# Linear attention and a mixture of experts on one core: the start of the pipeline and the last group rearranged

## The reference

```
q, k = exp(split_heads(x Wq' + bq)), exp(split_heads(x Wk' + bk));  v = split_heads(x Wv' + bv)   # 16 heads of 8
kv = cumsum(k outer v);  k1 = cumsum(k)
out = (q . kv) / sum(q * k1);   x = layernorm(x + merge_heads(out) Wo' + bo)
s = sigmoid(x gate_w');  choice = s + gate_bias;   4 groups of 8 experts: keep the 2 groups
    with the largest sum of their top 2, then the top 8 experts; weights s / sum(s) * 2.5
routed = sum over the 8 chosen of weight * down_e( silu(gate_e x) * up_e x )      # 32 experts, width 64
shared = down_s( silu(gate_s x) * up_s x )                                         # width 128
x = layernorm(x + routed + shared)
```

## Time and profile before

| | us |
|---|---|
| median of 3 runs | 462.77 (462.74 to 463.14) |
| the profiled execution | 463.29 |
| its span in the profile | 461.5 |
| PE busy in the span | 424.0 (92%) |
| DVE, POOL, ACT busy | 347.4, 282.4, 273.3 |

### The profile page before, as it was taken

How to read it: one execution, slowest core, us unless ns; L and a number is a source line. 1 busy time by engine, 2 the same in 40 slices (tenths; PEclk the granted TensorE clock), 3 DMA queues, 4 the chain that set the end, 5 groups by cost and what they waited for, 6 DMA issues and landing times.

```text
span 461.5 us, 10791 instructions
## 1 busy us (share of the span) xinstructions
PE 424.0 (92%) x3954; PEld 324.8 (70%) x3954; DVE 347.4 (75%) x909; ACT 273.3 (59%) x530; POOL 282.4 (61%) x208
## 2 busy tenths in 40 slices
PE   5855799999999999999999999999999999899982
PEld 3733587778867787778877787778877787578761
DVE  2678548797878968797878968796878968777652
ACT  3835334963587546963587546963587546555642
POOL 2565236864676557864677557764677557757781
PEclk9989589999999999999999999999999999999996
DMA  7400544346440823446340923446440913466500
GB/s 233 187 1 1 147 92 90 92 97 141 93 113 7 197 69 82 91 103 135 91 116 12 202 68 74 90 104 134 91 116 9 200 41 81 91 134 129 121 11 23
DMA packets 28660, 45.08 MB, mean 98 GB/s; under 512 B 1984, under 2 KB 10304, under 8 KB 28224
## 3 DMA queue, kind: packets, MB, share of 16 engines
q1 hardware_dynamic: 28608, 44.40, 41.2%
HBM read 41.77 MB, written 2.62 MB: 96 GB/s over the span
## 4 chain that ended last, share of the span: by engine, by line
PE 40%; DVE 32%; issue 12%; POOL 8%; ACT 2%; DVEq 1%; ACTq 0%; POOLq 0%
PE bank L326 39%; DVE units L866 7%; POOL units L958 5%; DVE stats L741 2%; DVE hidden_lo L721 2%; POOL rstd L977 2%; DVE top_of_group L782 2%; DVE x L753 2%; DVE bank L775 1%; ACT hidden_hi L584 1%; DVE replaced L814 1%; DVE out_sb L878 1%; DVE k_sum L847 1%; DVE probs L731 1%; DVE kv_blocks L836 1%
## 5 line engine op out<-in xcount | busy, mean ns | idle before, releaser
L958 POOL TENSOR_TENSOR units<-units,weight_wide 128x512 f32<-128x512 f32 x128 | 174.3, 1367 | 130.5 <-DVE units L866 115.9
L602 ACT ACTIVATE units<-bank 128x512 f32<-128x512 f32 x136 | 80.7, 594 | 79.2 <-PE bank L326 78.9
L866 DVE TENSOR_TENSOR units<-bank,units 128x512 f32<-128x512 f32 x136 | 92.9, 683 | 35.1 <-PE bank L326 28.0
L584 ACT ACTIVATE hidden_hi<-units 128x512 fp32r<-128x512 f32 x136 | 86.1, 634 | 53.7 <-POOL units L958 47.7
L721 DVE TENSOR_TENSOR hidden_lo<-units,hidden_hi 128x512 fp32r<-128x512 f32 x112 | 97.7, 873 | 19.6 <-ACT hidden_hi L584 18.8
L326 PE MATMUL bank<-x_hi,gate_hi 128*128 128x512 f32 x136 | 62.1, 457 | 2.0 <-DVE units L866 1.6
L326 PE MATMUL bank<-hidden_hi,down_hi 128*128 128x512 f32 x136 | 55.0, 404 | 1.7 <-DVE hidden_lo L721 1.7
L326 PE MATMUL bank<-x_hi,up_hi 128*128 128x512 f32 x136 | 54.7, 403 | 1.8 <-ACT units L602 1.8
L326 PE MATMUL bank<-x_lo,gate_hi 128*128 128x512 f32 x136 | 54.6, 401 | 0.0
L326 PE MATMUL bank<-x_hi,gate_lo 128*128 128x512 f32 x136 | 54.4, 400 | 0.0
L326 PE MATMUL bank<-x_hi,up_lo 128*128 128x512 f32 x136 | 54.1, 398 | 0.0
(11 more groups left out here) (107 smaller groups left out, 670.8 us busy)
## 6 DMA issues: line engine op xcount, KB each, us to landing
weight_wide<-weight_d SPq DMA_DIRECT2D x62, 512.0 KB, 6.7
xT<-xT_in SPq DMA_DIRECT2D x8, 256.0 KB, 6.8
x_tok<-x_in SPq DMA_DIRECT2D x8, 256.0 KB, 6.9
out_dram<-out_sb SPq DMA_DIRECT2D x8, 256.0 KB, 2.3
weight_wide<-up_in SPq DMA_DIRECT2D x1, 1088.0 KB, 9.0
up_raw<-up_in SPq DMA_DIRECT2D x1, 1088.0 KB, 11.0
down_raw<-down_in SPq DMA_DIRECT2D x1, 1088.0 KB, 13.2
weight_d<-weightT SPq DMA_DIRECT2D x8, 64.0 KB, 1.6
```

The lines of the kernel that those rows point to most:

```text
L584: nc.scalar.activation(hidden_hi[place(n, g)][:, :], units[place(n, g)][:, :], ACT.Copy).then_inc(hidden_hi_done, 1)
L602: nc.scalar.activation(units[place(n, g)][:, :], up_banks[2 * n % 3][:, :], ACT.Silu).then_inc(silu_done, 1)
L866: V.tensor_tensor(units[place(n, g)][:, :], up_banks[(2 * n + 1) % 3][:, :], units[place(n, g)][:, :], ALU.mult).then_inc(gated_done, 1)
L958: G.tensor_tensor(units[place(n, g)][:, :], units[place(n, g)][:, :], weight_wide[:, (n - 1) % (2 * PIECE), :], ALU.mult).then_inc(hidden_ ...
```

## The change

Four things change in the prologue. The scans of f = 1 (`k_totals(1)`) move on DVE from slot 8 of mid to slot 14, behind the routing and the first two gated products, and `q_times_totals(1)` moves on POOL from slot 10 to slot 13. POOL makes the low parts of the gate and up weights in two pieces each (nine blocks, then eight), and PE's first `up` waits for the first pieces only. Block 0's high and low parts move from slot 1 to slot 2. PE gets products into the output bank that nobody reads (`keep_warm`), 6 + 2 + 1 + 4 + 1 + 3 + 2 of 256 columns at seven places ahead of its waits.

In the steady state `masked_states(f)` moves ahead of `k_totals(f)`, both now in slot 14 (for f > 1). In the group without front (m = 7) the transpose of the routing exponentials moves on PE from slot 10 to slot 11.

In the last group the shared block comes last, the routed ones one slot earlier, and weight pieces 2 and 3 are loaded in slots 4 and 7. Its tail goes in two halves: two `yT` copies, two pairs of transposes into two banks, two residual additions, and in the end ACT normalises two tiles and DVE the two others, each half with a store of its own.

```
+EARLY_BLOCKS = 9
+WARM = {"x1": 6, "x1T": 2, "up": 1, "weight": 4, "den": 3, "between": 2}
         def ready_blocks(n, g):
-            if g == 0 and n in (2, 3):
-                return (1, 2) if n == 3 else ()
+            if g == 0 and n in (1, 2, 3):
+                return ((), (0,), (1, 2))[n - 1]
+        def block_at(n, g):
+            return n if g < GROUPS - 1 else (n + 1) % BLOCKS
...
@@ SP
-                if ffn and n in (5, 9):
-                    load_wide(2 + (n - 5) // 4, g, u)
+                late = (5, 9) if g < GROUPS - 1 else (4, 7)
+                if ffn and n in late:
+                    load_wide(2 + late.index(n), g, u)
+                if g == GROUPS and n == 8:
+                    for h, (done, count) in enumerate(((last_done, 1), (out_done, 2 * GROUPS - 1))):
...                                                  # one store for tiles 2, 3, then one for tiles 0, 1
@@ PE
-                if g == 0 and n == 0:
-                    pe.wait_ge(gate_split, 2)
-                    pe.wait_ge(up_split, 2)
+                if g == 0 and n in (0, EARLY_BLOCKS):
+                    pe.wait_ge(gate_split, 2 if n == 0 else 3)
+                    pe.wait_ge(up_split, 2 if n == 0 else 3)
+            def keep_warm(count):
+                for _ in range(count):
+                    mm(y_bank[:, 0:256], wqT, attn_w[:, 0:256])
...     # called: up(1), up(2) of group 0 ("up"); m = 0: ahead of the waits for x1 (slot 9), x1T (10), the expert
...     # weights (14); m = 1: after the wait for q times totals (slot 0, "den"), ahead of slot 2 ("between")
-                if mid and not front and n == 10:
+                if mid and not front and n == (10 if m == 0 else 11):
                     turn_exponentials(m)
@@ DVE
-                if m == 0 and mid and n == 8:
+                if m == 0 and mid and n == 14:
                     k_totals(1)
+                if front and f > 1 and n == 14:
+                    masked_states(f)
                 if front and f != 1 and n == 14:
                     k_totals(f)
-                if front and f != 1 and n == 15:
+                if front and f == 0 and n == 15:
                     masked_states(f)
+            def last_rows(t, u):                     # for the last group, in slot 4
+                for h, c in enumerate(HALVES):
+                    dve.wait_ge(y_turned, t + 1 + h)
+                    V.tensor_tensor(out_sb[half h], (work_bank, o_bank)[h][:, c], x1[u][half h], ALU.add)
...                                                  # bn_stats of the half; then aggregate, variance, negated mean
+                dve.wait_ge(rstd2_done, t + 1)
+                for i in (2, 3):
+                    last = V.tensor_scalar(out_sb[:, i, :], out_sb[:, i, :], mean_var2[:, i, 0:1], rstd2[:, i:i + 1],
+                                           ALU.subtract, ALU.mult)
+                last.then_inc(last_done, 1)
@@ POOL
-                if mid and m == 0 and n == 10:
+                if mid and m == 0 and n == 13:
                     q_times_totals(1)
                 if g == -2 and n == 16:
                     rows_and_bias(0)
-                    G.tensor_tensor(gate_lo[:, :], gate_raw, gate_hi[:, :].bitcast(F32), ALU.subtract
+                    weight_lows(gate_lo, gate_raw, gate_hi, gate_split, EARLY_COLS)
+                    weight_lows(up_lo, up_raw, up_hi, up_split, EARLY_COLS)
+                    weight_lows(gate_lo, gate_raw, gate_hi, gate_split, LATE_COLS)
-                if g == -1 and mid and n == 7:
-                    G.tensor_tensor(up_lo[:, :], up_raw, up_hi[:, :].bitcast(F32), ALU.subtract
+                if g == -1 and mid and n == 9:
+                    weight_lows(up_lo, up_raw, up_hi, up_split, LATE_COLS)
```

More of the change, by code:

```diff
@@ L27 @@
 RING = 4
+EARLY_BLOCKS = 9
+EARLY_COLS, LATE_COLS = slice(0, 128 * EARLY_BLOCKS), slice(128 * EARLY_BLOCKS, 128 * BLOCKS)
+WARM = {"x1": 6, "x1T": 2, "up": 1, "weight": 4, "den": 3, "between": 2}
+HALVES = (slice(0, GROUP // 2), slice(GROUP // 2, GROUP))
 OUT_SLOTS = (7, 8)
@@ L257, in slot @@
                     sp.dma_start(down_raw, down_d).then_inc(down_loaded, 16)
-                if tail and n == 8:
+                if g == GROUPS and n == 8:
+                    for h, (done, count) in enumerate(((last_done, 1), (out_done, 2 * GROUPS - 1))):
+                        tiles, at = slice(2 - 2 * h, 4 - 2 * h), (GROUPS - 1) * GROUP + 256 * (1 - h)
+                        sp.wait_ge(done, count)
+                        sp.sem_inc(apart, 1)
+                        sp.dma_start(out_d[at:at + 256, :].rearrange("(a p) c -> p a c", p=128),
+                                     out_sb[:, tiles, :]).then_inc(out_stored, 16)
+                if tail and n == 8 and g < GROUPS:
                     t = g - 1
@@ L367, in down @@
                     pe.wait_ge(y_copied, reached(g))
-                cols, h = slice(128 * n, 128 * n + 128), place(n, g)
+                cols, h = slice(128 * block_at(n, g), 128 * block_at(n, g) + 128), place(n, g)
                 mm(y_bank[:, :], down_hi[:, cols], hidden_hi[h][:, :], start=n == 0, stop=False)
@@ L422, in slot @@
                     down(BLOCKS - LAG, g - 1)
+                if ffn and g == 0 and n in (1, 2):
+                    keep_warm(WARM["up"])
                 if ffn:
@@ L427, in slot @@
                 if mid and n == 10:
+                    if m == 0:
+                        keep_warm(WARM["x1T"])
                     pe.wait_ge(x1T_copied, reached(m + 1))
@@ L467, in slot @@
                 if mid and n == 2:
+                    if m == 1:
+                        keep_warm(WARM["between"])
                     between_chunks(m, 0)
@@ L489, in slot @@
                 if mid and n == 9:
+                    if m == 0:
+                        keep_warm(WARM["x1"])
                     pe.wait_ge(x1_done, reached(m + 1))
@@ L537, in slot @@
                 if mid and n == 14:
+                    if m == 0:
+                        keep_warm(WARM["weight"])
                     pe.wait_ge(weight_done, reached(m + 1))
@@ L592, in slot @@
                     act.wait_ge(y_turned, reached(t))
-                    nc.scalar.activation(yT[:, :], y_bank[:, :], ACT.Copy).then_inc(y_copied, 1)
+                    for c in (HALVES if t == GROUPS - 1 else (slice(0, GROUP),)):
+                        nc.scalar.activation(yT[:, c], y_bank[:, c], ACT.Copy).then_inc(y_copied, 1)
                 if ffn:
@@ L682, in slot @@
                         high_part(b, g)
-                if tail and n in OUT_SLOTS:
+                if tail and n in OUT_SLOTS and (g < GROUPS or n == OUT_SLOTS[0]):
                     t = g - 1
@@ L873, in slot @@
                     V.reciprocal(inv_den[:, :], den_cols[:, :]).then_inc(inv_done, 1)
-                if tail and n == 4:
+                if tail and n == 4 and g < GROUPS:
                     t = g - 1
@@ L885, in slot @@
                     V.tensor_scalar(neg_mean2[:, :], mean_var2[:, :, 0], -1.0, None, ALU.mult).then_inc(neg_mean2_done, 1)
+                if g == GROUPS and n == 4:
+                    last_rows(g - 1, 1 - u)
                 if mid and n == 5:
@@ L941, in rows_and_bias, with weight_lows @@
                                 ).then_inc(x_bias_done, 1)
+            def weight_lows(low, raw, high, split, cols):
+                pool.wait_ge(split, 1)
+                G.tensor_tensor(low[:, cols], raw[:, cols], high[:, cols].bitcast(F32), ALU.subtract
+                                ).then_inc(split, 1)
             def q_times_totals(f):
```

62 lines of the change are left out of this document (42 added, 20 removed).

## The result

The changed kernel takes 467.74 us (median of 10 runs, 466.69 to 470.18); the kernel before took 463.18 beside it. The ratio is 1.011, with a 95% interval of 1.008 to 1.013: slower by 1.1%, where 2.1% faster was forecast. The profiled execution took 467.51.

The account below looks back on a forecast made before the run. PE was taken to bound the middle of the run, with gains where it waits: fill, group gaps, drain. 463.29 - 7.6 - 1.3 + 0.5 + 0.3 - 1.15 = 454.0 us, median 453.5, range 450 to 458.5.

Parts of the forecast that it names:

- The scans: Prologue, DVE: the two moved scans, free of POOL's hold on the port, cost 1.3 us; ends 1.3 and 5.6.
- Prologue to `up(3)`: From the start to `up(3)`: clock full, `up(3)` at 53.1 instead of 59.48, gain 7.6 us, bounds 5.0 and 8.6.
- What the unread products cost: Prologue, PE: products fill idle time and hold the clock; four ahead of the weights' transposes delay these by 0.5 us.
- four rivals: POOL wins port, 457 (0.20); scans stay 5.6 us, 460 (0.08); clock not held, 460 (0.05); long scans, low clock, 465 (0.04).
- PE idle after 53 for POOL or a DMA: After the prologue: a sign that the forecast is wrong, PE waiting after 53 us for POOL or a data transfer.
- Steady state: Six groups: PE's waits for masked chunk sums go, slot 16's gated product may shift; -1.3 us, ends -2.9 and +0.6.
- The tie at slot 16: Steady state: DVE's low part and POOL's unit ready near 99.05; DVE first saves PE 0.45, POOL first loses 0.1 a group.
- Turn of m = 7: Group m = 7, PE: nine matmuls first, exponentials turned 0.5 us later; costs +0.5, bounds 0 and 0.6.
- Last group: Shared block last: slot 4 about 1.9 us later, partly won back at the end; net +0.3, ends -0.8 and +1.9.
- the win at the end: End of last group: POOL is one unit of 1.3 us ahead, and ACT's last high part needs DVE alone.
- Tail: After the last `down`: halves overlap, ACT does two rows; -1.15 us, ends -0.7 and -1.4, second store 0.1 behind the first.
- the first rival: Every group's port goes to POOL, and the last group's fill is not won back: 457.5 us, median 457, chance 0.20.

Follow-up runs that it names:

- the kernel without products: The changed kernel with all unread products removed (all counts in `WARM` at 0), against the kernel before: 461.85 us, ratio 0.996.
- The kernel with small loads: The changed kernel with every instruction kept but fewer bytes in each spread weight load from group 1 on: 458.98 us, ratio 0.992 against the kernel before.
- the 512-column kernel: The changed kernel with 10 unread products of 512 columns in place of 19 of 256: 464.67 us, ratio 1.005 against the kernel before.
- the one with masked sums first: Prologue and tail by halves without unread products (459.08 us), plus masked states ahead of the totals in groups 0 to 5: 460.01 us, ratio 0.9940.

## Why the prediction was wrong, point by point

- **The scans.** Right: 1.27 us for 1.3.
- **Prologue to `up(3)`.** Right: 52.53 for 53.1, and 8.0 gained for 7.6, with the clock full. In the kernel with the prologue alone the same gain stands (8.3 at 54.5 us).
- **What the unread products cost.** This is the step that failed. I counted them as time on PE in idle stretches, 0.5 at most, and looked for their price in the stretch where they stand. Their price is that they are instructions: 76 of them move every later block edge of PE's program, and the blocks of four edges then come too late behind loads. By the table of delays this took 1.8 + 4.4 + 3.8 + 0.5 = 10.5 us, more than the gain of 8.0, at places that the change does not touch. None of the four rivals had it. The page before has the queue, at 0.5% of the DMA engines, and I passed over it.
- **"Wrong" signs I had named.** "PE idle after 53 for POOL or a DMA" was near: it was a DMA, but not of data.
- **Steady state.** The tie at slot 16 was seen, and it went to POOL. By the Trainium skill's rule (SBUF — State Buffer, section "Who interferes with whom") the holder keeps the port to its end; the low part of 1.62 beside the unit agrees. I took -1.3 between the ends -2.9 and +0.6; it was +0.9 by the creep, outside both ends.
- **Turn of m = 7.** +0.3 for +0.5, by the table of delays; the kernel without products, which has the same turn, shows the same 0.3 there. Not tried by itself.
- **Last group.** +1.8 for +0.3, inside the bound of 1.9. The fill's cost was mis-sized little (2.3 for 1.9); what failed is the win at the end, 0.5 for 1.6. I had said that the last high part would need DVE alone. But on ACT it stands behind the high part of the last routed block, and that one waited 1.79 us for POOL's last unit (452.60 to 454.27), which could only begin when DVE's product ended at 452.52.
- **Tail.** -1.4 for -1.15, at the bound of -1.4. Counted from the end of the last `down` (457.37), as the 6.9 was, the stores are issued at 5.5 and 6.0 us, where I had put the last at 5.8: the second came 0.55 behind the first and not 0.1. The smaller last store then ended sooner than the whole one had.

Without the edges the forecast's own terms, with the measured sizes, give 463.3 - 8.0 + 0.9 + 0.3 + 1.8 - 1.4 = 456.9 in the profiled execution's terms; with the 10.5 of the edges it is 467.4, and 467.51 was measured. So even without the edges the forecast of 454.0 would have missed by 3 us, on the side of the first rival (457.5), whose two conditions, POOL first at slot 16 and a fill that is not won back, both held. The kernel with small loads, which keeps one stop, measured 459.0.

How early a block is asked for can be read in part. In every stop of these traces the packet that ended it was the one with the same place in the row (the sixteenth packet at the edge 4289, the twentieth at 5313), so packets and edges can be matched one by one. In the kernel after each packet started between 3.4 us before and 5.8 us after PE began the block just before the one that the packet brings, so no block came long ahead. What to look for is therefore a block that PE works off while loads hold the engines. But full engines alone are not enough. At 101.4 and at 153.0 us of after a packet ran in the middle of loads at 100% of the engines, for instance in this DMA view, 153 to 154 us:

```profile
q1 hardware_dynamic: 102, 0.20, 100.4%
q8 instruction: 1, 0.02, 8.2%
```

Left open: what let those packets pass and held the others until the loads' end, and so how to foresee a stop without a run; why a stop is followed by a half clock in some runs and not in others (after 2.80 it was, after 2.87 in the 512-column kernel it was not; of the ten stops of about 2 us and more in all traces nine were followed by one); and whether the spread of single kernels (the one with masked sums first ran from 456.6 to 463.1) is this edge and this clock, as the stop at 1217 suggests.

## What to carry to other kernels

Count the instructions that an edit adds to an engine's program, not only their time, and look where the block edges then fall against the large loads: the fetches share the DMA engines with them. In the page this is the "instruction" queue; in the timeline it is a stop "<-issue" in the middle of like instructions, at an index that repeats modulo 256. When a kernel gets slower at places that were not touched, compare equal instructions of both traces first. Work that is only there to keep a clock up moves the edges least as few wide instructions: six products of 512 columns took the time from 459.08 to 457.13 here, 19 of 256 had cost more than the whole change gained.

## What the runs showed of the hardware that I had not expected

- A packet of PE's instructions is 16 KB for 256 instructions. From the packet's start to PE's next instruction it takes 2.4 to 2.6 us (208.5 to 210.93, 264.8 to 267.38, 104.1 to 106.59, 222.5 to 224.93), although the loads have ended; over all stops of these traces 2.2 to 2.9.
- With the DMA engines at 92% for 10 us no packet of PE's instructions passed; with them at 30% it passed in time. It isn't a strict rule: two others passed at 100%, as shown above.
- A bare semaphore increment in PE's program took 0.153 us in both kernels that have them: their starts run from 0.82 to 28.17 us for 180 and from 0.82 to 12.30 for 76. The first matmul came later by less than that (0.11 to 0.135 each), since before it began only at some 4 us. Matmuls of 512 columns start 0.23 us apart, so an increment costs two thirds of one.
- A stop of PE of 2 to 3 us in the middle of the run can bring the clock down to half behind it, for 3.4 us in the kernel after, which cost another 1.4 and 1.7 us.
